# One ScalarE pass per head for the cross attention's softmax in a two-layer decoder

## The reference

```python
xn = (x - mu) * jax.lax.rsqrt(var + LN_EPS) * ln_gamma + ln_beta
q, k, v = split_heads(xn @ Wq), *map(split_heads, jnp.split(context @ Wkv, 2, axis=-1))
dots = jnp.einsum('bhnd,bhmd->bhnm', q, k) * DIM_HEAD ** (-0.5)
dots = jnp.where(mask, dots, -jnp.inf)
attn = jax.nn.softmax(dots, axis=-1)          # 16 heads x 64 context rows per token
out = jnp.einsum('bhnm,bhmd->bhnd', attn, v)
return out.transpose(0, 2, 1, 3).reshape(...) @ Wo + bo
```

## Time and profile before

| | us |
|---|---|
| median of 3 runs | 1379.32 |
| lowest and highest | 1376.8, 1381.81 |
| the profiled execution, its own time | 1384.11 |
| its span, first to last instruction | 1382.5 |
| PE busy | 1083.8 (78%) |
| DVE busy | 988.9 (72%) |
| ACT busy | 480.3 (35%) |
| POOL busy | 387.4 (28%) |

### The profile page before, as it was taken

The page is one execution under the profiler, slowest core; times in us unless marked ns, Lnnn a source line. Parts: engine busy times, 40 slices in busy tenths (PEclk is TensorE's granted clock), DMA queues, the critical chain, the costliest instruction groups (busy, mean ns, idle before and its releaser), DMA issues. The chain is left out here.

```text
span 1382.5 us, 20435 instructions
## 1 busy us (share of the span) xinstructions
PE 1083.8 (78%) x6769; PEld 903.0 (65%) x6770; DVE 988.9 (72%) x1817; ACT 480.3 (35%) x1066; POOL 387.4 (28%) x525
## 2 busy tenths in 40 slices
PE   1588888866576789999516498898989989898987
PEld 0477777744165578888403387787777878687887
DVE  5789999855866012222299999999999999999621
ACT  0111121122063322322101164655555554655453
POOL 1112222200022400000320053636254353636342
PEclk9889999987798599999757699999999999999999
DMA  9014520000001866666270000000000000000000
GB/s 278 18 69 164 191 99 9 1 1 1 0 1 61 335 225 249 226 226 233 79 323 5 1 1 1 9 0 0 8 0 8 0 8 0 0 8 0 9 9 9
DMA packets 23972, 98.86 MB, mean 72 GB/s; under 512 B 3728, under 2 KB 15184, under 8 KB 17584
## 3 DMA queue, kind: packets, MB, share of 16 engines
q1 hardware_dynamic: 16080, 73.60, 14.5%
q10 hardware_dynamic: 5200, 17.37, 3.8%
q0 software_dynamic: 2640, 7.21, 1.5%
HBM read 87.96 MB, written 21.76 MB: 79 GB/s over the span
## 5 line engine op out<-in xcount | busy, mean ns | idle before, releaser
L1998 PE MATMUL bank<-n_hA_hi_reduced,ffn_h 128*128 128x256 f32 x512 | 128.1, 293 | 12.5 <-POOL n_hA_lo_reduced L1818 8.6
L1998 PE MATMUL bank<-n_hB_hi_reduced,ffn_h 128*128 128x256 f32 x512 | 126.1, 290 | 5.9 <-ACT n_hA_lo L2129 4.5
L1998 PE MATMUL bank<-n_hA_lo_reduced,ffn_h 128*128 128x256 f32 x512 | 124.6, 286 | 0.0
L1998 PE MATMUL bank<-n_hB_lo_reduced,ffn_h 128*128 128x256 f32 x512 | 120.6, 279 | 0.0
L1998 PEld LDWEIGHTS bank<-n_hA_hi_reduced,ffn_h 128*128 128x128 f32 x512 | 100.1, 195 | 16.1 <-POOL n_hA_lo_reduced L1818 14.7
L2245 DVE TENSOR_TENSOR d_prod<-d_qk,d_xT 128x512 f32<-128x512 f32 x128 | 104.6, 857 | 0.5
L1998 PEld LDWEIGHTS bank<-n_hB_hi_reduced,ffn_h 128*128 128x128 f32 x512 | 96.6, 189 | 9.3 <-ACT n_hA_lo L2129 5.9
L1998 PEld LDWEIGHTS bank<-n_hA_lo_reduced,ffn_h 128*128 128x128 f32 x512 | 100.4, 196 | 0.2
L1639 DVE TENSOR_TENSOR e_y<-bank,e_b 128x256 f32<-128x256 f32 x23 | 9.8, 425 | 123.9 <-PE bank L1569 123.9
L1998 PEld LDWEIGHTS bank<-n_hB_lo_reduced,ffn_h 128*128 128x128 f32 x512 | 96.6, 189 | 1.8 <-issue 1.7
L1614 ACT ACTIVATE e_hT<-bank,e_b 128x128 f32<-128x128 f32 x184 | 52.6, 368 | 128.5 <-PE bank L1557 128.5
(11 more groups left out here) (344 smaller groups left out, 2634.3 us busy)
## 6 DMA issues: line engine op xcount, KB each, us to landing
e_w<-in_W SPq DMA_DIRECT2D x23, 1024.0 KB, 6.0
ffn_weights<-in_F ACTq DMA_DIRECT2D x2, 5632.0 KB, 20.8
e_piece<-ffn_weights SPq DMA_DIRECT2D x11, 1024.0 KB, 4.9
ffn_h<-ffn_weights SPq DMA_DIRECT2D x2, 4096.0 KB, 18.7
ffn_w<-ffn_weights SPq DMA_DIRECT2D x3, 1024.0 KB, 7.2
expert_rows<-zero ACTq DMA_DIRECT2D x1, 2944.0 KB, 10.3
e_xs<-expert_rows SPq DMA_DIRECT2D x23, 128.0 KB, 4.5
expert_out<-e_y POOLq DMA_DIRECT2D x23, 128.0 KB, 2.0
```

The lines of the kernel that those rows point to most:

```text
L1998: last = nc.tensor.matmul(F[f % 2][:, 0:PAIR], weight(w[:, k, f * P:(f + 1) * P], fast), operand(src[part][1][:, k, :], fast), start=(c == ...
```

## The change

DVE takes the maxima straight into a new tile `score_max`, multiplies them by -1/8, and hands over; the subtraction into `d_pr` and the sum per head are gone from DVE. ACT reads the scores from PSUM with one exponent pass per head, 16 passes of 128 x 64 in place of one of 128 x 1024, each with the head's scaled maximum as its bias (a column of 128 values) and with an accumulated sum into `score_sum`. DVE then takes the reciprocal of that sum and multiplies. ACT also waits now until the probabilities of the tile before have been turned, since it has become the first writer of `d_pr`. PE's and POOL's programs are unchanged.

```diff
             def score_exp(k, i, b):
-                act.wait_ge(q["sub"], k + 1)
-                nc.scalar.activation(pr[:, :], pr[:, :], ACT.Exp, scale=D2 ** -0.5).then_inc(q["sexp"], 1)
+                act.wait_ge(q["max"], k + 1)
+                after("prob_turned", k)
+                for h in range(H2):
+                    last = nc.scalar.activation(pr[:, h * SC:(h + 1) * SC], bank_s[h // 8][:, h % 8 * SC:(h % 8 + 1) * SC],
+                                                ACT.Exp, bias=score_max[b][:, 1, h:h + 1], scale=D2 ** -0.5,
+                                                accum_out=score_sum[b][:, h:h + 1])
+                last.then_inc(q["sexp"], 1)
...
-            def scores_less_max(k, i, b):
+            def scores_max(k, i, b):
                 heads = lambda ap: ap.rearrange("p (h s) -> p h s", s=SC)
                 v.wait_ge(q["score_done"], k + 1)
                 for n in range(2):
-                    link(V.tensor_reduce(mx[b][:, 0, 8 * n:8 * n + 8], heads(bank_s[n][:, :]), AX.X, ALU.max))
-                for n in range(2):
-                    last = V.tensor_tensor(heads(pr[:, 512 * n:512 * (n + 1)]), heads(bank_s[n][:, :]),
-                                           spread(mx[b][:, 0, 8 * n:8 * n + 8], 2, SC), ALU.subtract)
-                last.then_inc(q["sub"], 1)
+                    link.behind(V.tensor_reduce(score_max[b][:, 0, 8 * n:8 * n + 8], heads(bank_s[n][:, :]), AX.X, ALU.max),
+                                1 - n)
+                V.tensor_scalar(score_max[b][:, 1, :], score_max[b][:, 0, :], -D2 ** -0.5, None,
+                                ALU.mult).then_inc(q["max"], 1)
 
             def probabilities(k, i, b):
                 p3 = pr[:, :].rearrange("p (h s) -> p h s", s=SC)
                 v.wait_ge(q["sexp"], k + 1)
-                link(V.tensor_reduce(mx[b][:, 1, 0:H2], p3, AX.X, ALU.add))
-                link(V.reciprocal(mx[b][:, 1, 0:H2], mx[b][:, 1, 0:H2]))
-                V.tensor_tensor(p3, p3, spread(mx[b][:, 1, 0:H2], 2, SC), ALU.mult).then_inc(q["prob"], 1)
+                link(V.reciprocal(score_sum[b][:, :], score_sum[b][:, :]))
+                V.tensor_tensor(p3, p3, spread(score_sum[b][:, :], 2, SC), ALU.mult).then_inc(q["prob"], 1)
```

More of the change, by code:

```diff
@@ L1712, in stage_layer1 @@
     mx = both("mx", [P, 2, 2 * H])
+    score_max = both("score_max", [P, 2, H2])
+    score_sum = both("score_sum", [P, H2])
     pr = late("d_pr", [P, FF], F32)
@@ L1727, in stage_layer1 @@
     names = ("x_var", "x_pow", "x3", "x3_turned", "x3T", "qkv_done", "v_copied", "pre", "exp", "attn_var", "attn_pow",
-             "xn", "xn_turned", "xnT", "score_done", "sub", "sexp", "prob", "prob_turned", "probT", "out_done",
+             "xn", "xn_turned", "xnT", "score_done", "max", "sexp", "prob", "prob_turned", "probT", "out_done",
              "out_var", "out_pow", "x5", "x5_kept", "x5_turned", "x5T", "split")
@@ L2065, in _, with after @@
         def _(act):
+            def after(name, count):
+                if not (isinstance(count, int) and count <= 0):
+                    act.wait_ge(q[name], count)
             def x3_copied(k, i, b):
@@ L2353, in trip @@
                 tile(contexts, n - 1, 0, 1)
-                tile(scores_less_max, n - 2, 1)
+                tile(scores_max, n - 2, 1)
                 tile(contexts, n - 1, 0, 2)
@@ L2381, in trip @@
                 tile(contexts, n - 1, 1, 2)
-                tile(scores_less_max, n - 1, 0)
+                tile(scores_max, n - 1, 0)
                 tile(contexts, n - 1, 1, 3)
@@ L2408, in _ @@
                 trip(n)
-TRIP_LINKS = 110
+TRIP_LINKS = 108
 def build(nc, ins, out):
```

## The result

The changed kernel takes 1406.62 us (median of 4 runs, 1406.5 to 1413.07); the kernel before, with its runs beside these, 1380.57 (1376.8 to 1386.08). The ratio is 1.0203, with a 95% interval of 1.0172 to 1.0234: about 2% slower. The spans of the profiled executions are 1404.9 and 1382.5 us, 22.4 apart, and it is these that the traces can account for.

A forecast was written before the change was run, and what follows sets the result against it. DVE was taken to bound the kernel, with PE close behind. PE's chain +34, tiles 0 and 1 about -1 and the clock +8 gave +41 us on 1379.3, so 1420 us, range 1370 to 1452.

The forecast's parts named there:

- What bounds, and the turn of it: DVE sets the pace, 73.7 of 77.9 us busy per pair; PE some 9 us behind takes over through ACT.
- the signs that I had named: Passes 6 to 7 us per tile, PE waits about 5 us 14 times, a pair takes 82 to 84 us.
- What DVE loses: Softmax work on DVE: two subtractions and the sum less, 2.36 us per tile, 37.8 us for 16 tiles.
- The length of the block: Sixteen exponent passes with sums on ACT, per tile: 0.41 us per head, 6.5 us in total.
- its bounds: Block on ACT: 3.4 us if the sum is free, 8.4 if passes don't overlap and a further instruction writes it.
- The ledger of stalls: PE's waits around ACT's exponents: added 14E - 26.3, given back 31; the end moves by 14E - 57, +34 us.
- E: Total time of a tile's sixteen exponent passes on ACT, taken as 6.5 us.
- nothing hides it: Exponent right behind its table load, ahead of GELUs of units 0 and 1: PE stalls E - 1.2 per pair.
- Given back: PE's waits for DVE that vanish: 10.2 for `d_x`, 3.6 for `d_pr`, 17 of 19.8 for `d_r`; sum 31 us.
- The clock: PE's granted clock after stalls: one more slow stretch per pair, at most 15 us; taken as 8 us.
- Tiles 0 and 1: Tiles with no feed-forward work about: 0.65 us gained each, 1.3 in all.
- the deciding point: Length of ACT's sixteen passes, E = 4.1 us or 0.26 us per head; below it the kernel is faster.

## Why the prediction was right, and where its terms were off

- **What bounds, and the turn of it.** Right. DVE set the pace, PE followed 9 us behind, and with the change PE's chain through ACT took over. The experiment that holds ACT alone shows it. Of the signs that I had named, the places came out and the sizes did not: a pair takes 80.9 us and not 82 to 84, and PE's stalls behind the exponents are about 3 us each and not 5.
- **What DVE loses.** Near: forecast 37.8 us, measured 30.5 of busy time. Most of the difference is the other attention's products, which became slower; the changed kernel's groups from 715 us to the end:

```profile
L2257 DVE TENSOR_TENSOR d_prod<-d_qk,d_xT 128x512 f32<-128x512 f32 x120 | 102.3, 892 | 0.5
L2269 DVE TENSOR_TENSOR d_prod<-d_qk,d_T 128x512 f32<-128x512 f32 x120 | 89.3, 784 | 10.6 <-POOL x_tok L1809 10.3
```

  In the kernel before the same two were busy for 99.5 and 85.9 us (mean 869 and 755 ns), so 6.2 us came on top. Why they slowed I did not establish.
- **The length of the block.** Mis-sized, inside its bounds: I took 0.41 us per head and it is 0.291. The lower bound for the pass alone was met (3.4 us forecast for sixteen, 3.38 measured). The further instruction exists, as the upper bound had it, but it overlaps pass and next pass and adds 0.09 us per head to passes that come every 0.2 us; I had put 0.1 on passes that don't overlap (0.315). Here the error is 14 x 1.65 = 23 us of the forecast.
- **The ledger of stalls.** Right in its total: with E = 4.85 it gives 14 x 4.85 - 26.3 = 41.6 us of added stalls, measured 43.2 - 4.5 = 38.7. The halves are less good, and their errors oppose each other. Behind b=0 it gives 7 x 3.65 = 25.6 us and 19.6 were measured, so something did hide 0.9 us of each, against my "nothing hides it"; behind b=1 it gives 16.1, and 23.6 - 4.5 = 19.1 were measured. Given back: 31 forecast, 28.6 measured (10.2 + 3.6 + 14.8). The limit on what the wait for `d_r` gives back was right; 0.84 us was left of it each time, and I had said about 1.
- **What the ledger lacked.** PE's other waits grew: for POOL from 8.6 to 11.6, for `turned_x3` from 9.2 to 10.9, and 3.4 us new at `first`. That is 8 us which my sum did not have. The first two of these waits were in the trace before; I had left them out of the earlier trace rows when I called nearly all of PE's waits DVE's.
- **The clock.** Direction right, size about: PE's busy time rose by 10.7 us where I had put 8. It has moved, not only grown. PE had idled 3.71 us before 942 and then ran at 0.50; now it idles 0.84 us there and keeps 1.00, and the slow stretches follow the stalls at the GELUs. Busy by stretch and PEclk, changed kernel:

```profile
926.90:931.00 4.10, 4.10 (x22) 4.10 (x22) 2.97 (x5) 1.46 (x4) 1.77 (x3) 0.58 0.00 0
943.00:947.00 4.00, 3.60 (x28) 3.40 (x29) 3.65 (x11) 3.31 (x4) 1.73 (x3) 1.00 0.00 0
973.50:977.50 4.00, 3.96 (x34) 3.96 (x35) 2.65 (x5) 1.57 (x4) 2.81 (x4) 1.00 0.19 66
1007.20:1011.20 4.00, 3.95 (x18) 3.95 (x19) 2.82 (x4) 0.86 (x3) 1.76 (x3) 0.50 0.00 0
```

  Behind stalls of 3.0 and 3.4 us (926.9, 1007.2) the granted clock was 0.58 and 0.50 for 4 us, behind one of 3.2 us (973.5) it stayed at 1.00: PE made 34 matmuls there in the time of 18 to 22. From 800 us on, thirteen of the fourteen stalls for ACT are 3.0 us or longer, and eleven of the thirteen are followed by 4 us at 0.50 to 0.63; so is one wait for POOL of 4.4 us. In the kernel before, seven waits are followed so (six for `d_r`, one for POOL, at 0.50 to 0.66). Five more such stretches at my 2.2 us give an estimate of 11 us, beside the 10.7 measured. My 8 was half of fifteen, for want of better.
- **Tiles 0 and 1.** The forecast of 1.3 us was too small for the same reason as the block: with 4.85 us DVE waits 0.2 us there in all. From the maxima of tile 0 to those of tile 2 it took 71.3 us and not 75.9, and the kernel with the form there alone is 6 us faster.

The sum with these sizes: stalls +38.7, given back -28.6, other waits +8.1, PE slower +10.7, tiles 0 and 1 -4.6, together +24.3, against 22.4 in the spans. The forecast of +41 was 15 us above the medians' +26. The block's length alone made it 23 us too high, and what the ledger lacked took part of that back: with E = 4.85 my own sum gives 14 x 4.85 - 57 - 1.3 + 8 = +18, some 8 us too low. So the step that was off is the block's length, and that the miss stayed at 15 us is in part luck. What I had marked as the deciding point, a length at which the change turns from loss to gain, was not located for this form, only bracketed: the kernel without accumulated sums gains at 3.4 us, with less work taken from DVE, and the changed kernel loses at 4.85.

The page "ScalarE: Activation LUTs" of the Trainium skill (What ACT_TABLE_LOAD costs) gave an estimate of 3.9 us for the passes. Here the measurement decides: sixteen passes without sums took 3.38 us, 0.5 us less than by the page. With the sums they took 4.85 us.

## What to carry to other kernels

Before work is moved to an engine with idle time, look at what is queued behind the place where it lands and who waits for that: ACT was busy 53% of a pair and had 36 us to spare, but not at the two places where PE needs its next GELU. Write the moved work's length as a variable, follow it through each engine that waits, and find the length at which the sign turns; then move only as much as fits. Here half of the heads fit: with all heads in the two tiles beside which no GELUs run (0.6%) and half of them in the others, the kernel gained 1.1%, where the form in full lost 2%.

## What the runs showed of the hardware

- An accumulated sum on ACT is an ACTIVATION_READ_ACCUMULATOR behind each pass; with 64 columns from PSUM and a bias column, pass and read come every 0.291 us (sixteen in 4.85 us), the pass alone every 0.204 us (sixteen in 3.38 us, in the kernel without accumulated sums). I had expected more overhead for it.
- A Copy of one column on ACT, from SBUF to SBUF, takes 0.096 us back to back (25 in 2.41 us, 40 in 3.80), less than the 0.15 us which I had worked out from wider passes. Two experiments were too small for that reason.
